# Convolution attention: the first head pair's maxima and the split of wp taken from the start of the attention phase into the end of the projections

## The chip, the cores and the metric

One core of a Trainium2 chip (trn2). The metric is the device time of one execution in microseconds; lower is better. The kernel before took 3423.76 us, the median of three runs (3422.56 to 3425.62).

## The reference

Input x is (8, 768, 32, 32) float32, here used as 8 batches of 768 channels by 1024 positions, with four 768x768 weights. Group normalisation without scale (32 groups, eps 1e-5), then

```python
q, k, v = conv1x1(Wq), conv1x1(Wk), conv1x1(Wv)      # of the normalised x, 12 heads of 64 channels
scores = einsum('bhdn,bhdm->bhnm', q, k) / sqrt(64)
attn = softmax(scores, axis=-1)
out = einsum('bhnm,bhdm->bhdn', attn, v)
return x + einsum('oc,bchw->bohw', Wp, out)
```

## The kernel before, in words

The kernel keeps float32 precision with products of two parts: each operand is split into a rounded part (fp32r, "hi") and the rest ("lo"), and three of the four products are summed. It has two phases, each one block in which every engine runs a program of its own; a barrier stands between them, and tensors of the first phase are freed for the second.

**project_phase.** Eight batches (the first and the last written out, the six between them in a loop), each of two halves of 512 positions. A half is 20 groups: 6 of queries, 6 of keys (18 matmuls of 128x512 each, line 240), 8 of values (18 of 128x384). The groups go round a ring of RING = 4 PSUM banks and of four stage buffers. For a query or key group ACT rounds the bank to the stage's first half (line 290), DVE puts the rest in the second (line 380); for a value group DVE copies (line 385). SP stores to DRAM (q_dram, k_dram at line 175, v_dram at line 179), each after a wait for `lo_done`. The weights lie in `w_hi` and `w_lo`, the normalised input in `xn_hi` and `xn_lo`, with an index for the half. In half 0 the second half of the same batch is normalised on ACT and split on DVE, behind groups 0 to 5, and in half 1 the next batch's first half. The x of the next batch is loaded to `x_raw` in half 0, before group 6's stores. In the last batch there is no next batch. The phase ends when SP has seen all stores land; then comes the barrier (line 49).

**attend_phase.** 48 head pairs (2 heads of 64 channels on the upper and lower 64 rows), each of MT = 8 steps t of 128 keys. For the softmax the kernel needs each query's maximum first. For pair p+1 this is made beside pair p, in UNITS = 16 units: `scores_by_query` (line 731) is two matmuls 64x512, one for each head, to the two banks `rows`, and `unit_max` (line 902) a DVE reduction over both. Unit n waits for the reduction of unit n-1 (`max_done`). When all 16 are done, `join` reduces the halves, turns the result with four 32x32 transposes (lines 908 to 914), and SP sends it as a row to `top` (line 573), one row for each head, whose other rows are zero. `scores_by_key` (line 746) waits for `top_in` at t = 0 and takes, for each step, eight matmuls for each half, the last two of which add the maxima as a product of `ones_r` and `top`. ACT takes the exponent to `p_all` (line 862), POOL sums (line 702), `values` on PE (line 759) multiplies by v. From pair LAG = 8 on, `output` (line 769) multiplies the normalised heads by wp.

PE's order in pair p, step 0, is: unit 0 of pair p+1, then (but for p = 0) the last values of p-1, then unit 1, then scores by key, then unit 2.

**The start of attend_phase before.** SP loads q and k of pair 0, v of pair 0, q and k of pair 1, then wp in five pieces into tensors that are not used yet (lines 562, 563, 567, 644). PE runs pair 0's 16 units, in turn to `rows` and `heads`; DVE clears `ones_r`, `top` and `neg_max` (lines 945 to 947), reduces the 16 units and turns them; SP sends the maxima. ACT rounds wp (line 888), POOL makes its second part (line 710), and SP waits for that (`wp_lo_done`) before it goes on to pair 2's loads; ACT waits for it before the first exponent.

Of the kernel before, what the change touches and what calls it, by code (L numbers as in the profile page):

```python
# [5 lines left out]
F32 = mybir.dt.float32  # L6
# [6 lines left out]
P = 128  # L13
BANK = 512
# [5 lines left out]
def f32(ap):  # L20

    return ap.bitcast(F32)
# [12 lines left out]
def project_phase(nc, S, x, weights, avg_in, q_dram, k_dram, v_dram, psum):  # L35
# [13 lines left out]
    with ExitStack() as ctx:  # L49
# [6 lines left out]
        w_hi = sb("w_hi", [P, 3, KT, C], F32R)  # L56
        w_lo = sb("w_lo", [P, 3, KT, C], F32R)
        x_raw = sb("x_raw", [P, KT, N])
        xn = sb("xn", [P, 2, BANK])
        xn_hi = sb("xn_hi", [P, 2, KT, BANK], F32R)  # L60
        xn_lo = sb("xn_lo", [P, 2, KT, BANK], F32R)
        stage = sb("stage", [P, RING, 2 * BANK], F32R)
        raw = sb("raw", [P, 2, C])
        early = f32(stage[:, :, :]).rearrange("p r n -> p (r n)")[:, 0:EARLY * C].rearrange("p (k o) -> p k o", k=EARLY)
        avg = sb("avg", [P, P])
# [12 lines left out]

        const_in = sem("const_in")
# [25 lines left out]

        NEXT_AT = (0, 2)
# [36 lines left out]
        def _(sp):  # L143
# [39 lines left out]
            for r in range(RING):  # L183
                sp.wait_ge(stored[r], 16 * STORES[r] * S.HALVES * B)

        @block.tensor
        def _(pe):
# [11 lines left out]
            def first_groups():  # L199
                for kt in range(KT):  # L200
                    pe.wait_ge(xn_lo_done, kt + 1)
                    pe.wait_ge(w_hi_done, kt + 1)
                    for g in range(RING):
                        w = w_hi[:, 0, kt, g * P:(g + 1) * P]
                        pe.matmul(psum[:, g, :], w, xn_hi[:, 0, kt, :], start=(kt == 0), stop=False)
                        pe.matmul(psum[:, g, :], w, xn_lo[:, 0, kt, :], start=False, stop=False)
                for g in range(RING):
                    for kt in range(KT):
                        if g == 0:
                            pe.wait_ge(w_lo_done, kt + 1)  # L210
                        mm = pe.matmul(psum[:, g, :], w_lo[:, 0, kt, g * P:(g + 1) * P], xn_hi[:, 0, kt, :], start=False, stop=(kt == KT - 1))
                    mm.then_inc(group_done, 1)

            def project(b, half, last):
# [4 lines left out]
                for g in range(RING if begun else 0, PER_HALF):  # L219
# [3 lines left out]
                    for kt in range(KT):  # L223
# [4 lines left out]
                        a, z = xn_hi[:, half, kt, :], xn_lo[:, half, kt, :]  # L228
                        if g < 2 * KT:
                            w, cols = g // KT, slice(g % KT * P, (g % KT + 1) * P)  # L230
                            wa, wz = w_hi[:, w, kt, cols], w_lo[:, w, kt, cols]
                            parts = [(wa, a), (wa, z), (wz, a)]
                        else:
                            nt, cg = (g - 2 * KT) // 2, (g - 2 * KT) % 2
                            t, cols = slice(nt * P, (nt + 1) * P), slice(cg * VC, (cg + 1) * VC)
                            va, vz = w_hi[:, 2, kt, cols], w_lo[:, 2, kt, cols]
# [4 lines left out]
                    mm.then_inc(group_done, 1)  # L241
                    if half == 0 and not last:
# [15 lines left out]
        def _(act):  # L258
            def high_weights(n):
# [4 lines left out]
                act.copy(w_hi[:, n // KT, n % KT, :], weight_rows(n)).then_inc(w_hi_done, 1)  # L264
# [762 lines left out]
```

## Time and profile before

| what | value |
|---|---|
| median of three runs | 3423.76 us (3422.56 to 3425.62) |
| the profiled execution | 3425.97 us |
| its span (first to last instruction) | 3424.1 us |
| granted clock of TensorE, mean | 0.994 |
| busy share PE / DVE / ACT / POOL | 97% / 52% / 32% / 53% |

All stretches are given in us from the start of the span. The projections take the span to about 1222.6 us, attention the rest. A clock of 1.00 is 2.4 GHz, 0.50 is 1.2 GHz. Matmuls overlap, so the time from the start of one to the start of the next tells more than the length of one.

### The profile page before, as it was taken

How to read it: one execution, taken by the hardware profiler on the slowest of the kernel's cores; microseconds unless marked ns; L12 is line 12 of the kernel's file. 1: busy time of each engine (PE TensorE's matmuls, PEld its weight loads, DVE VectorE, ACT ScalarE, POOL GpSimd, SP SyncE). 2: the span in 40 equal slices, each digit the busy share in tenths (PEclk: the TensorE clock that was granted, in tenths of full speed). 3: DMA queues.
4: the chain of work that ended last, by engine and by line, in shares of the span. 5: the costliest groups of instructions: out<-in, count | busy, mean ns of one | idle time of the engine just before them, and what ended most of it. 6: DMA issues, size and time to landing. Idle time of an engine off the chain costs nothing.

```text
span 3424.1 us, 51515 instructions
## 1 busy us (share of the span) xinstructions
PE 3332.4 (97%) x18272; PEld 2252.0 (66%) x18272; DVE 1784.3 (52%) x2417; ACT 1089.0 (32%) x1944; POOL 1831.8 (53%) x789
## 2 busy tenths in 40 slices
PE   7999999999999979999999999999999999999999
PEld 6888888888888854445555555555555555555557
DVE  5333323333332147775666666666666666666652
ACT  3111111111111114553344444444434444444441
POOL 2000000000000039998888888888888888888883
PEclk9999999999999989999999999999999999999999
DMA  6233333323333332334434434344344344343434
GB/s 233 103 135 111 141 140 115 141 99 135 110 141 111 111 139 88 129 109 157 152 119 154 134 123 159 125 152 158 124 152 148 124 142 146 130 155 124 155 105 166
DMA packets 221695, 461.86 MB, mean 135 GB/s; under 512 B 22960, under 2 KB 73008, under 8 KB 220208
## 3 DMA queue, kind: packets, MB, share of 16 engines
q1 hardware_dynamic: 221488, 459.16, 38.5%
q8 instruction: 123, 2.02, 0.3%
q14 instruction: 84, 0.69, 0.1%
HBM read 259.06 MB, written 199.62 MB: 134 GB/s over the span
## 4 chain that ended last, share of the span: by engine, by line
PE 50%; issue 5%; DVE 5%; DMA 3%; POOL 1%; SPq 1%; ACT 1%; DVEq 0%; ACTq 0%; POOLq 0%
PE psum L746 17%; PE psum L759 16%; PE psum L769 9%; PE psum L731 6%; DVE half_max L902 2%; PE psum L828 1%; DMA recip_rows<-compact 1%; DVE quads L932 1%; DMA top<-turned 1%; DVE compact L935 1%; POOL sums L702 1%; ACT p_all L862 1%; SPq L603 0%; DMA o_parts<-o_lo 0%; POOL o_lo L690 0%
## 5 line engine op out<-in xcount | busy, mean ns | idle before, releaser
L702 POOL TENSOR_TENSOR sums<-sums,p_all 128x1024 f32<-128x1024 f32 x576 | 1350.6, 2378 | 0.0
L902 DVE TENSOR_REDUCE half_max<-psum 128x2 f32<-128x1024 f32 x768 | 935.5, 1220 | 536.4 <-PE psum L731 518.9
L862 ACT ACTIVATE p_all<-psum 128x512 f32<-128x512 f32 x1536 | 793.0, 602 | 948.8 <-PE psum L746 944.1
L759 PE MATMUL psum<-p_all,v 128*64 128x512 f32 x3072 | 743.4, 605 | 0.0
L746 PE MATMUL psum<-q,k 64*128 64x512 f32 x4608 | 672.5, 397 | 13.2 <-DMA top<-turned 10.4
L710 POOL TENSOR_TENSOR wp<-sums,wp 128x1536 fp32r<-128x1536 f32 x1 | 3.5, 3450 | 1177.2 <-ACT wp L888 1177.2
L746 PEld LDWEIGHTS psum<-q,k 64*128 64x128 f32 x4608 | 427.4, 186 | 127.8 <-ACT p_all L862 33.6
L240 PE MATMUL psum<-xn_hi,w_hi 128*128 128x512 f32 x1128 | 439.8, 390 | 1.1 <-DVE stage L380 1.1
L240 PE MATMUL psum<-xn_hi,w_lo 128*128 128x512 f32 x1128 | 439.1, 389 | 0.0
L240 PE MATMUL psum<-xn_lo,w_hi 128*128 128x512 f32 x1128 | 439.0, 389 | 0.0
L290 ACT CAST stage<-psum 128x512 fp32r<-128x512 f32 x192 | 112.4, 587 | 961.4 <-PE psum L240 951.7
L759 PEld LDWEIGHTS psum<-p_all,v 128*64 128x64 f32 x3072 | 186.3, 136 | 345.9 <-issue 295.5
L380 DVE TENSOR_TENSOR stage<-psum,stage 128x512 fp32r<-128x512 f32 x192 | 132.5, 691 | 537.2 <-ACT stage L290 537.0
L731 PE MATMUL psum<-k,q 64*128 64x512 f32 x1536 | 355.8, 459 | 45.3 <-DVE half_max L902 28.6
L702 POOL TENSOR_TENSOR sums<-p_all 128x1024 f32<-128x1024 f32 x96 | 226.4, 2379 | 314.2 <-ACT p_all L862 314.2
L731 PEld LDWEIGHTS psum<-k,q 64*128 64x128 f32 x1536 | 145.7, 186 | 362.3 <-DVE half_max L902 285.9
L769 PE MATMUL psum<-a,wp 128*128 128x512 f32 x1512 | 367.7, 397 | 0.1
L769 PEld LDWEIGHTS psum<-a,wp 128*128 128x128 f32 x1512 | 277.4, 188 | 122.0 <-issue 33.3
L746 PE MATMUL psum<-top,ones_r 64*128 64x512 f32 x1536 | 303.0, 389 | 0.0
L240 PE MATMUL psum<-w_hi,xn_hi 128*128 128x384 f32 x768 | 257.3, 335 | 0.0
L240 PE MATMUL psum<-w_hi,xn_lo 128*128 128x384 f32 x768 | 256.8, 334 | 0.0
L240 PE MATMUL psum<-w_lo,xn_hi 128*128 128x384 f32 x768 | 256.7, 334 | 0.0
(78 smaller groups left out, 2570.1 us busy)
## 6 DMA issues: line engine op xcount, KB each, us to landing
q_parts<-stage SPq DMA_DIRECT2D x192, 256.0 KB, 2.2
k_parts<-stage SPq DMA_DIRECT2D x192, 256.0 KB, 2.3
q<-q_parts SPq DMA_DIRECT2D x48, 1024.0 KB, 5.0
k<-k_parts SPq DMA_DIRECT2D x48, 1024.0 KB, 7.3
a<-o_parts SPq DMA_DIRECT2D x84, 512.0 KB, 7.7
v_rows<-stage SPq DMA_DIRECT2D x128, 192.0 KB, 2.1
v<-v_rows SPq DMA_DIRECT2D x48, 512.0 KB, 4.6
recip_all<-recip_rows SPq DMA_DIRECT2D x96, 256.0 KB, 3.9
```

The lines of the kernel that those rows point to most:

```text
L240: mm = pe.matmul(out, lhs, rhs, start=(kt == 0 and n == 0), stop=(kt == KT - 1 and n == 2))
L290: act.copy(stage[:, r, 0:BANK], psum[:, r, :]).then_inc(hi_done, 1)
L380: dve.tensor_tensor(stage[:, r, BANK:2 * BANK], psum[:, r, :], f32(stage[:, r, 0:BANK]), ALU.subtract).then_inc(lo_done, 1)
L702: pool.tensor_tensor(sums[:, m % 2, i, :], first, p_all[:, i, n, :], ALU.add).then_inc(added, 1)
L731: mm = pe.matmul(to[:, i, :], queries, k[part, e, 0, h * BANK:(h + 1) * BANK], start=True, stop=True)
L746: mm = pe.matmul(psum[:, SCORE_BANKS[2 * h + i], :], left, right, start=(c == 0), stop=(c == 3))
L759: mm = pe.matmul(heads[part, h, :], v[:, e, t, part], p_all[:, i, (m * MT + t) % EXPS, cols], start=(t == 0), stop=(t == MT - 1))
L769: mm = pe.matmul(bank, wp[:, wpart, kt, ot * P:(ot + 1) * P], a_of[kt][:, apart, :], start=first, stop=final)
L828: mm = pe.matmul(psum[:, LAST_BANKS[n], :], wp[:, wpart, kt, ot * P:(ot + 1) * P], a_last[kt][:, apart, half * BANK:(half + 1) * BANK], st ...
L862: act.activation(p_all[:, i, (m * MT + t) % EXPS, h * BANK:(h + 1) * BANK], psum[:, SCORE_BANKS[2 * h + i], :], ACT.Exp, scale=SCALE).then ...
L902: dve.tensor_reduce(half_max[:, :, t, h], of, AX.X, ALU.max, negate=True).then_inc(max_done, 1)
L932: dve.transpose(quads[:, b, :], part[b * SQUARE:(b + 1) * SQUARE, :, :].rearrange("r i c -> r (i c)")).then_inc(quads_done, 1)
```

## The change

The two phases stay two blocks with a barrier. What the second phase's start did is moved into the last half (half 1 of batch 7) of the first, in memory that the last half no longer uses.

- A class `Shared` holds tensors that live through both phases. The weights are now three tensors (queries, keys, values), each with its hi and lo part, and the normalised input two tensors, one for each half. `w_first` (queries) becomes wp; `x_first` (half 0's input) holds slot 0 of q, k and `top`, and slot 1 of `top`; `w_second` (keys) holds slots 1 and 2 of q and k and slot 2 of `top`. The semaphores that pair 0's maxima use are shared too.
- SP: wp is loaded to `x_raw` in the last batch's half 0 before group 6's stores. q and k of pair 0 are loaded at the head of the last half, after a wait for all stores before it; those of pair 1 before group 12's store. Before group 19's store, SP waits for the turned maxima and sends them.
- PE: `maximum_unit` n comes behind group n + 3 of the last half, into PSUM banks 6 and 7, from `x_first`.
- DVE: behind group n + 3's work the reduction of unit n, and behind unit 15 the turn, in the free rows of the buffer `raw`.
- ACT: six copies of wp (768 columns each) behind groups 6 to 11. POOL: the clearing of `top`, and six subtractions for wp's second part.
- From the start of attend_phase go: the loads of q and k of pairs 0 and 1, of wp, the 16 units and reductions, the turn, the memset of `top`, wp's rounding and splitting, and the waits for `wp_lo_done`. v of pair 0 is still loaded there.

The order of PE's instructions around the barrier before. Line 240 is a projection matmul; 731 are units (the 32 matmuls of pair 0's 16 units and the 4 of pair 1's first two stand in one row, x36), 746 scores by key:

```order
L240 MATMUL psum<-w_hi,xn_lo 128x384
L49 UNCONDITIONAL_BRANCH
L718 UNCONDITIONAL_BRANCH
L731 MATMUL psum<-k,q 128x512 x36
L746 MATMUL psum<-q,k 128x512 x6
L746 MATMUL psum<-top,ones_r 128x512 x2
```

And of the change, where line 340 is a projection matmul, 310 a unit of pair 0, 829 a unit of pair 1, 844 scores by key:

```order
L310 MATMUL psum<-x_first 128x512 x2
L340 MATMUL psum<-w_third,x_second 128x384 x18
L106 UNCONDITIONAL_BRANCH
L816 UNCONDITIONAL_BRANCH
L829 MATMUL psum<-w_second 128x512 x4
L844 MATMUL psum<-x_first 128x512 x6
L844 MATMUL psum<-x_first,ones_r 128x512 x2
```

The 32 matmuls now stand in pairs between groups of 18; the last unit has one group behind it.

SP's queue from the last batch on, before:

```order
L175 DMA q_parts<-stage 128x512 x12
L175 DMA k_parts<-stage 128x512 x12
L179 DMA v_rows<-stage 128x3x128 x8
L49 UNCONDITIONAL_BRANCH
L556 UNCONDITIONAL_BRANCH
L562 DMA q<-q_parts 128x2x1024
L563 DMA k<-k_parts 128x2x1024
L567 DMA v<-v_rows 128x1024
L562 DMA q<-q_parts 128x2x1024
L563 DMA k<-k_parts 128x2x1024
L644 DMA sums<-in_wp 128x2x768
```

And of the change, from the last half on (the load of wp stands a half earlier):

```order
L71 DMA x_first<-q_parts 128x2x1024
L72 DMA x_first<-k_parts 128x2x1024
L263 DMA q_parts<-stage 128x512 x12
L263 DMA k_parts<-stage 128x512 x12
L71 DMA w_second<-q_parts 128x2x1024
L72 DMA w_second<-k_parts 128x2x1024
L267 DMA v_rows<-stage 128x3x128 x7
L77 DMA x_first<-turned_first 1x8x128 x2
L267 DMA v_rows<-stage 128x3x128
L106 UNCONDITIONAL_BRANCH
L669 UNCONDITIONAL_BRANCH
L678 DMA v<-v_rows 128x1024
```

Two pairs of loads moved ahead of stores of the last half, and the maxima ahead of its last store.

The diff, cut to its core:

```diff
+class Shared:
...
+        self.w_first = sb("w_first", [P, 2, S.KT, S.C])
+        self.w_second = sb("w_second", [P, 2, S.KT, S.C])
+        self.x_first = sb("x_first", [P, 2, S.KT, BANK])
+        second = self.w_second.rearrange("p a k o -> p (a k o)")
+        first = self.x_first.rearrange("p a k n -> p (a k n)")
+        slots = [first[:, 0:SLOT], second[:, 0:SLOT], second[:, SLOT:2 * SLOT]]
+        self.q = [t.rearrange("p (s a n) -> p s a n", s=2, a=2)[:, 0] for t in slots]
+        self.k = [t.rearrange("p (s a n) -> p s a n", s=2, a=2)[:, 1] for t in slots]
+        self.top = [first[:, SLOT:SLOT + N], first[:, SLOT + N:SLOT + 2 * N], second[:, 2 * SLOT:2 * SLOT + N]]
...
+def load_pair(sp, shared, q_dram, k_dram, p, e):
+    ch = bass.ds(p * P, P)
+    sp.dma_start(f32(shared.q[e]), q_dram[:, ch, :].rearrange("s p n -> p s n")).then_inc(shared.qk_in[e], 16)
+    sp.dma_start(f32(shared.k[e]), k_dram[:, ch, :].rearrange("s p n -> p s n")).then_inc(shared.qk_in[e], 16)
+
+
+def send_maxima(sp, shared, turned, e, MT, DH):
+    for i in range(2):
+        sp.dma_start(f32(shared.top[e][i * DH:i * DH + 1, :]).rearrange("a (t n) -> a t n", t=MT),
+                     f32(turned[i * MT:(i + 1) * MT, :])).then_inc(shared.top_in, 16)
+
+
+def turn_maxima(dve, shared, p, neg_max, flipped, turned, half_max, MT):
+
+    dve.tensor_reduce(neg_max[:, 0:2 * MT].rearrange("p (i t) -> p i t", i=2), half_max[:], AX.X, ALU.min).then_inc(shared.joined, 1)
+    dve.wait_ge(shared.joined, p + 1)
+    for b in range(TURNS):
+        part = slice(b * SQUARE, (b + 1) * SQUARE)
+        dve.transpose(flipped[:, part], neg_max[part, :]).then_inc(shared.flips, 1)
+    dve.wait_ge(shared.flips, TURNS * (p + 1))
+    dve.tensor_reduce(turned[:], flipped[0:2 * MT, :].rearrange("r (n a) -> r n a", a=1), AX.X, ALU.min).then_inc(shared.neg_done, 1)
...
+        w_third = sb("w_third", [P, 2, KT, C], F32R)
+        w_parts = (shared.w_first, shared.w_second, w_third)
+        w_hi, w_lo = [[w[:, part, :, :] for w in w_parts] for part in range(2)]
...
+        turned = sb("turned_first", [2 * S.MT, P], F32R)
...
+        half_max = rest[:, 0:4 * S.MT].rearrange("p (i t h) -> p i t h", i=2, t=S.MT)
+        neg_max = rest[:, 4 * S.MT:4 * S.MT + SQUARE]
+        flipped = rest[0:SQUARE, 4 * S.MT + SQUARE:4 * S.MT + SQUARE + P]
+        wp_raw = x_raw.rearrange("p k n -> p (k n)")[:, 0:KT * C].rearrange("p (k o) -> p k o", k=KT)
+        rows = psum[:, 6:8, :]
...
+        UNIT_AT = 3
+        UNITS = 2 * S.MT
+        LAST_UNIT = B * S.HALVES - 1
...
+                        if last and half == 0 and g == NEXT_AT[0] + KT:
+                            sp.wait_ge(xn_made, B * S.HALVES * KT)
+                            sp.dma_start(wp_raw, wp_rows.rearrange("(k p) o -> p k o", p=P)).then_inc(wp_in, 16)
+                        if last and half == 1 and g == 0:
+                            sp.wait_ge(group_done, LAST_UNIT * PER_HALF)
+                            for r2 in range(RING):
+                                sp.wait_ge(stored[r2], 16 * STORES[r2] * S.HALVES)
+                            load_pair(sp, shared, q_dram, k_dram, 0, 0)
+                        if last and half == 1 and g == 2 * KT:
+                            sp.wait_ge(group_done, LAST_UNIT * PER_HALF + 2 * KT)
+                            load_pair(sp, shared, q_dram, k_dram, 1, 1)
+                        if last and half == 1 and g == PER_HALF - 1:
+                            sp.wait_ge(shared.neg_done, 1)
+                            sp.wait_ge(zero_done, 1)
+                            send_maxima(sp, shared, turned, 0, S.MT, DH)
...
             for r in range(RING):
                 sp.wait_ge(stored[r], 16 * STORES[r] * S.HALVES * B)
+            sp.wait_ge(shared.top_in, 32)
...
+            def maximum_unit(unit):
+                t, h = unit // 2, unit % 2
+                if unit == 0:
+                    pe.wait_ge(shared.qk_in[0], 32)
+                wait(pe, shared.max_done, unit)
+                for i in range(2):
+                    part = slice(i * DH, (i + 1) * DH)
+                    mm = pe.matmul(rows[:, i, :], shared.q[0][part, 0, t * P:(t + 1) * P], shared.k[0][part, 0, h * BANK:(h + 1) * BANK],
+                                   start=True, stop=True)
+                mm.then_inc(shared.rows_ready, 1)
...
+                    if last and half == 1 and 0 <= g - UNIT_AT < UNITS:
+                        maximum_unit(g - UNIT_AT)
...
+                        if last and half == 1 and 0 <= g - KT < KT:
+                            if g == KT:
+                                act.wait_ge(wp_in, 16)
+                            act.wait_ge(group_done, unit * PER_HALF + KT)
+                            act.copy(shared.w_first[:, 0, g - KT, :], wp_raw[:, g - KT, :]).then_inc(wp_hi_done, 1)
...
+            pool.wait_ge(group_done, LAST_UNIT * PER_HALF)
+            pool.memset(f32(shared.top[0]), 0.0).then_inc(zero_done, 1)
+            pool.memset(f32(shared.top[1]), 0.0).then_inc(zero_done, 1)
+            for kt in range(KT):
+                pool.wait_ge(wp_hi_done, kt + 1)
+                pool.tensor_tensor(shared.w_first[:, 1, kt, :], wp_raw[:, kt, :], f32(shared.w_first[:, 0, kt, :]),
+                                   ALU.subtract).then_inc(wp_lo_done, 1)
+            pool.wait_ge(group_done, LAST_UNIT * PER_HALF + 2 * KT)
+            pool.memset(f32(shared.top[2]), 0.0).then_inc(zero_done, 1)
...
+            def unit_max(unit):
+                t, h = unit // 2, unit % 2
+                if unit == 0:
+                    dve.wait_ge(w_lo_done, 3 * KT)
+                    dve.memset(neg_max, 0.0).then_inc(neg_clear, 1)
+                dve.wait_ge(shared.rows_ready, unit + 1)
+                dve.tensor_reduce(half_max[:, :, t, h], rows, AX.X, ALU.max, negate=True).then_inc(shared.max_done, 1)
...
+                        if last and half == 1 and 0 <= g - UNIT_AT < UNITS:
+                            unit_max(g - UNIT_AT)
+                            if g - UNIT_AT == UNITS - 1:
+                                dve.wait_ge(shared.max_done, UNITS)
+                                dve.wait_ge(neg_clear, 1)
+                                turn_maxima(dve, shared, 0, neg_max, flipped, turned, half_max, S.MT)
...
-        q = sb("q", [P, SLOTS, 2, N], F32R)
-        k = sb("k", [P, SLOTS, 2, N], F32R)
-        top = sb("top", [P, SLOTS, N], F32R)
+        q, k, top, wp = shared.q, shared.k, shared.top, shared.w_first
+        qk_in, top_in, rows_ready, max_done = shared.qk_in, shared.top_in, shared.rows_ready, shared.max_done
+        neg_done = shared.neg_done
...
-            load_qk(0, 0, 0)
             load_v(0, 0, 0)
-            load_qk(1, 1, 0)
-            for kts, buf in wp_raw:
-                sp.dma_start(buf, wp_rows[kts.start * P:kts.stop * P, :].rearrange("(k p) o -> p k o", p=P)).then_inc(wp_in, 16)
-            sp.wait_ge(set_done, SETS)
-            maxima(0, 0)
-            sp.wait_ge(wp_lo_done, len(wp_raw))
...
-            for n, (kts, buf) in enumerate(wp_raw):
-                pool.wait_ge(wp_hi_done, n + 1)
-                pool.tensor_tensor(wp[:, 1, kts, :], buf, f32(wp[:, 0, kts, :]), ALU.subtract).then_inc(wp_lo_done, 1)
-            pool.wait_ge(wp_lo_done, len(wp_raw))
...
-            for unit in range(UNITS):
-                scores_by_query(0, 0, None, unit, to=heads if unit % 2 else rows, taken=unit - 1)
...
-                    if known(p) and p == LAG and s == 0:
-                        pe.wait_ge(wp_lo_done, len(wp_raw))
...
-            act.wait_ge(wp_in, 16 * len(wp_raw))
-            for kts, buf in wp_raw:
-                act.copy(wp[:, 0, kts, :], buf).then_inc(wp_hi_done, 1)
-            act.wait_ge(wp_lo_done, len(wp_raw))
...
-            dve.memset(f32(top[:]), 0.0).then_inc(set_done, 1)
             dve.memset(neg_max[:], 0.0).then_inc(set_done, 1)
             dve.wait_ge(set_done, SETS)
-            for unit in range(UNITS):
-                unit_max(0, 0, unit, heads if unit % 2 else rows)
-            join(0, 0)
```

## Rows read from the trace of the kernel before

**Rows 1.** The page's part 1: busy us (share of the span) xinstructions.

```profile
PE 3332.4 (97%) x18272; PEld 2252.0 (66%) x18272; DVE 1784.3 (52%) x2417; ACT 1089.0 (32%) x1944; POOL 1831.8 (53%) x789
```

**Rows 2.** Windows, busy of PE, PEld, DVE, ACT, POOL, then clock, DMA, GB/s.

```profile
1220.00:1230.00 10.00, 2.64 (x16) 2.31 (x14) 3.49 (x5) 0.00 (x0) 0.00 (x0) 0.88 0.44 136
1230.00:1240.00 10.00, 4.40 (x12) 1.65 (x12) 5.50 (x5) 0.00 (x0) 0.00 (x0) 0.50 1.03 414
...
1250.00:1260.00 10.00, 5.63 (x22) 3.39 (x22) 6.40 (x11) 1.81 (x4) 8.53 (x5) 0.50 0.03 7
```

**Rows 3.** The chain of waits at the seam: start, us, what.

```profile
1226.27 7.28 DMA k<-k_parts
...
1234.50 18.20 DVE half_max L902 x16
...
1254.24 0.81 SPq L573
...
1255.09 1.76 DMA top<-turned
...
1256.89 3.78 PE psum L746 x16
1260.68 0.43 PE psum L731 x2
...
1295.07 1.23 PE psum L746 x8
```

**Rows 4.** The timeline at the seam: start, us, engine, line, what [idle before <-releaser].

```profile
1222.30 0.34 PE L240 MATMUL psum<-w_hi,xn_lo 128*128 128x384 f32 x1
1222.67 0.56 DVE L385 COPY stage<-psum 128x384 f32<-128x384 f32 x1 [2.57 <-PE psum L240]
1223.26 0.37 SPq L179 DMA_DIRECT2D v_rows<-stage  x1
1225.83 0.39 SPq L562 DMA_DIRECT2D q<-q_parts  x1
...
1226.67 2.62 DVE L946 MEMSET top<- 128x3072 f32 x1 [0.59 <-issue]
...
1233.59 1.22 PE L731 MATMUL psum<-k,q 64*128 64x512 f32 x4 [10.95 <-DMA k<-k_parts]
```

**Rows 5.** The timeline of DVE, one key group of the last half.

```profile
1198.31 0.69 DVE L380 TENSOR_TENSOR stage<-psum,stage 128x512 fp32r<-128x512 f32 x1 [3.39 <-ACT stage L290]
```

**Rows 6.** The page's part 6: one load of keys, KB, us to landing.

```profile
k<-k_parts SPq DMA_DIRECT2D x48, 1024.0 KB, 7.3
```

**Rows 7.** The timeline of PE at full clock, inside a steady head pair.

```profile
1782.61 0.50 PE L731 MATMUL psum<-k,q 64*128 64x512 f32 x2
1783.04 1.94 PE L759 MATMUL psum<-p_all,v 128*64 128x512 f32 x8
1784.91 4.38 PE L769 MATMUL psum<-a,wp 128*128 128x512 f32 x18
1789.22 0.50 PE L731 MATMUL psum<-k,q 64*128 64x512 f32 x2
```

**Rows 8.** The timeline of POOL, the last of wp's splits.

```profile
1256.72 1.81 POOL L710 TENSOR_TENSOR wp<-v,wp 128x768 fp32r<-128x768 f32 x1
```

**Rows 9.** The timeline of PE: pair 1's first unit, alone.

```profile
1252.84 0.80 PE L731 MATMUL psum<-k,q 64*128 64x512 f32 x2 [1.56 <-DVE half_max L902]
```

**Rows 10.** Windows of 1 us in which the clock fell or rose.

```profile
1227.00:1228.00 1.00, 0.00 (x0) 0.00 (x0) 1.00 (x1) 0.00 (x0) 0.00 (x0) 0.79 0.64 152
1261.00:1262.00 1.00, 1.00 (x10) 0.77 (x8) 0.86 (x1) 0.79 (x2) 0.00 (x0) 0.64 1.06 430
1562.00:1563.00 1.00, 0.00 (x0) 0.00 (x0) 0.00 (x0) 0.00 (x0) 0.13 (x1) 0.54 0.97 168
1568.00:1569.00 1.00, 1.00 (x8) 0.73 (x8) 0.73 (x1) 0.16 (x1) 0.00 (x0) 0.54 0.73 186
```

**Rows 11.** The timeline of PE around the second fall.

```profile
1563.26 0.93 PEld L746 LDWEIGHTS psum<-q,k 64*128 64x128 f32 x6 [3.99 <-DMA top<-turned]
```

More of the change, by code:

```diff
@@ L32, in __init__, with sb, sem @@
         self.NH = self.B * HEADS
-def project_phase(nc, S, x, weights, avg_in, q_dram, k_dram, v_dram, psum):
+SLOTS = 3
+SQUARE = 32
+TURNS = P // SQUARE
+class Shared:
+    def __init__(self, nc, S, ctx):
+        def sb(name, shape):
+            return ctx.enter_context(nc.sbuf_tensor(name, shape, F32R))
+        def sem(name):
+            return ctx.enter_context(nc.semaphore(name))
+        N, SLOT = S.N, 4 * S.N
+        self.w_first = sb("w_first", [P, 2, S.KT, S.C])
[7 more added lines that the diff above has]
+        self.top = [first[:, SLOT:SLOT + N], first[:, SLOT + N:SLOT + 2 * N], second[:, 2 * SLOT:2 * SLOT + N]]
+        self.qk_in = [sem(f"qk_in{s}") for s in range(SLOTS)]
+        self.top_in = sem("top_in")
+        self.rows_ready = sem("rows_ready")
+        self.max_done = sem("max_done")
+        self.joined = sem("joined")
+        self.flips = sem("flips")
+        self.neg_done = sem("neg_done")
@@ L203, in first_groups @@
                     for g in range(RING):
-                        w = w_hi[:, 0, kt, g * P:(g + 1) * P]
-                        pe.matmul(psum[:, g, :], w, xn_hi[:, 0, kt, :], start=(kt == 0), stop=False)
-                        pe.matmul(psum[:, g, :], w, xn_lo[:, 0, kt, :], start=False, stop=False)
+                        w = w_hi[0][:, kt, g * P:(g + 1) * P]
+                        pe.matmul(psum[:, g, :], w, xn_hi[0][:, kt, :], start=(kt == 0), stop=False)
+                        pe.matmul(psum[:, g, :], w, xn_lo[0][:, kt, :], start=False, stop=False)
                 for g in range(RING):
@@ L449, in attend_phase @@
         flipped = sb("flipped", [SQUARE, P])
-        turned = sb("turned", [2 * MT, 2, P], F32R)
+        turned = [sb(f"turned{n}", [2 * MT, P], F32R) for n in range(2)]
         flip = sb("flip", [P, N])
@@ L571, in maxima @@
                 sp.wait_ge(neg_done, p + 1)
-                for i in range(2):
-                    sp.dma_start(f32(top[i * DH:i * DH + 1, m % SLOTS, :]).rearrange("a (t n) -> a t n", t=MT),
-                                 f32(turned[i * MT:(i + 1) * MT, m % 2, :])).then_inc(top_in, 16)
+                send_maxima(sp, shared, turned[m % 2], m % SLOTS, MT, DH)
             def spread_recip(p):
@@ L721, in _, with scores_by_query @@
             PRODUCTS = [(kt, wpart, apart) for kt in range(KT) for wpart, apart in ((0, 0), (0, 1), (1, 0))]
-            def scores_by_query(p, m, u, unit, to=rows, taken=None):
+            def scores_by_query(p, m, u, unit):
                 t, h = unit // 2, unit % 2
@@ L727, in scores_by_query @@
                     pe.wait_ge(qk_in[e], 32 * (turn(p, m, u) + 1))
-                wait(pe, max_done, p * UNITS + unit if taken is None else taken)
+                wait(pe, max_done, p * UNITS + unit)
                 for i, part in enumerate(half_of):
-                    queries = q[part, e, 0, t * P:(t + 1) * P]
-                    mm = pe.matmul(to[:, i, :], queries, k[part, e, 0, h * BANK:(h + 1) * BANK], start=True, stop=True)
+                    queries = q[e][part, 0, t * P:(t + 1) * P]
+                    mm = pe.matmul(rows[:, i, :], queries, k[e][part, 0, h * BANK:(h + 1) * BANK], start=True, stop=True)
                 mm.then_inc(rows_ready, 1)
@@ L896, in _, with unit_max @@
         def _(dve):
-            def unit_max(p, m, unit, of=rows):
+            def unit_max(p, m, unit):
                 t, h = unit // 2, unit % 2
@@ L901, in unit_max @@
                     wait(dve, neg_done, p)
[L902 removed]
+                dve.tensor_reduce(half_max[:, :, t, h], rows, AX.X, ALU.max, negate=True).then_inc(max_done, 1)
             def join(p, m):
```

79 lines of the change are left out of this document (29 added, 50 removed).

## The prediction

> **What bounds the kernel now.** I read the page first, then the windows, then the chain of waits, then the timelines at the seam. PE is busy 97% of the span [rows 1], so little can be won except where PE stands still. The windows show where that is: the seam between the two phases. From 1220 to 1230 us PE works 2.64 us of 10, from 1230 to 1240 4.40, from 1250 to 1260 5.63, the last two at a granted clock of 0.50, which is 1.2 GHz [rows 2]. The chain says what the seam waits for, in order: the transfer of the first pair's keys (7.28 us, to 1233.54), sixteen row maxima on DVE (18.20 us), the turning of the maxima, their two transfers (the first issued at 1254.24, the second landing 1.76 us after 1255.09), and at 1256.89 the first scores by key [rows 3]. The last projection ends on PE at 1222.64 [rows 4]. So the seam, from the last projection to the first scores by key, is 1256.89 - 1222.64 = 34.25 us. From 1256.89 on the work is the same before and after the change, so its new length is the whole question.
>
> **What the change moves, and its price.** The sum follows the moment of the first score by key.
>
> 1. *The loads of pair 0 leave the seam.* They are issued on SP at the head of the last half, 16.3 us before their first use: a key or query group takes 0.69 + 3.39 = 4.08 us [rows 5], and the first unit stands behind the fourth. SP first waits for the stores of the half before. Such a store is issued 0.6 us after its group, and in the old seam issue, landing and barrier together took 1225.83 - 1223.26 = 2.57 us [rows 4], so SP goes on about 3.2 us into the half. Queries and keys need a median of 7.3 us [rows 6], which makes 11 us of the 16.3. Cost nothing; without that cover PE would wait for the difference. The stores of the half's first group, now behind these two DMAs in SP's queue, are only issued from 5 us on anyway. Pair 1's loads sit before the first value group, 27 us or more before their use.
>
> 2. *Sixteen units (two matmuls each) enter the last half on PE.* That time is added, since PE has no gap there. The nearest row is a unit between 128-row matmuls at full clock: 1783.04 - 1782.61 = 0.43 us [rows 7]. Cheapest would be 0.24, half of one of the eight pairs in 3.78 us at half clock [rows 3]. Dearest: the 18 matmuls ahead of a unit took 4.31 us [rows 7] against a projection group's 4.08, 0.23 more, so 0.66. I take 0.49, near the first row. 16 x 0.49 = 7.8 us; ends 3.8 and 10.6. The Trainium skill, TensorEngine Tiling (Array Packing), section Key Properties, says that changing the tiling mode drains the engine. If each unit then cost what a lone pair did, 0.80 us at half clock [rows 9], the sum would be 5.0 us dearer, a rival below; the row above shows 0.2 us over the bare pair, so the trace bears out a mild form only.
>
> 3. *Their maxima on DVE.* A unit's reduction takes 18.20 / 16 = 1.14 us in the old seam, and DVE is idle 3.39 us of each 4.08 [rows 5], 2.57 us of each 3.13 in value groups [rows 4]. Cost nothing: the next unit comes a group later, and PE is four banks ahead.
>
> 4. *wp.* One load of 2.36 MB, in the place where other batches load x; six copies on ACT and six splits on POOL of 1.81 us [rows 8], all idle then. They were beside the maxima before, the last split ending at 1258.53, so they pay back nothing either.
>
> 5. *The block's end.* Old: 1225.83 - 1222.64 = 3.19 us from PE's end to SP's first instruction behind the barrier. New: behind group 18 come unit 15 on PE, its maximum and the turn. From the reduction's end at 1252.70 to SP's issue at 1254.24 this took 1.54 us [rows 3]. So: unit 0.5, reduction 1.2, turn 1.5, two issues of 0.81; SP is free for the last value store 4.9 us behind group 18. The last group ends 0.49 + 3.13 = 3.6 us behind it, so the store goes 1.25 us after PE's end where it went 0.62 before [rows 4]. Then 2.57 us as before: 3.8 us, 0.6 more. The top rows land meanwhile (1.76 us after the second issue).
>
> 6. *The new block's start.* PE waits for two DVE memsets. Old DVE showed 0.59 us of issue gap before the second, which began 0.84 us after SP's first instruction [rows 4]; I take 1.0 us, without the 2.62 us memset of `top`, which is on POOL and hidden. Then unit 0 of pair 1, at half clock: 0.91 us to the reduction's start (1233.59 to 1234.50), 1.23 us of reduction and a step of 0.05, 2.2 us in all; then unit 1 and 0.43 us to the scores by key [rows 3]. The old seam had these two units as well, the first at 1252.84 [rows 9], spread around the turn.
>
> Sum: 7.8 + 3.8 + 1.0 + 2.2 + 0.4 = 15.2 us in place of 34.25, so 19.0 us less. The profiled execution took 3425.97 us with a span of 3424.1; less 19.0 is 3407.0. The median of the three runs is 3423.76, 2.2 below that execution, and the forecast is made against it: **3404.8 us**. Every number above is a difference, so the offset carries over.
>
> *The clock.* A window of 1 us at a mean of 0.79 was at full rate for 0.58 of it and at half for the rest, so the clock fell at 1227.58, 4.9 us after PE's last matmul; in the same way it rose at 1261.7, 4.8 us into the dense scores [rows 10]. At the other fall PE had stopped at 1563.26 - 3.68 = 1559.58 [rows 11]; the clock fell at 1562.1, 2.5 us later, and rose at 1568.9. The new PE stands still 4.8 us (3.8 + 1.0), then works thinly. I assume that it falls again and that the same half-speed stretch follows, so it adds nothing to the difference. What is late next is the barrier itself and the two memsets; from the first scores on, PE.
>
> **The rivals.**
>
> *The clock holds.* For it: 4.9 us of idleness in one case were needed, and the new stop is 4.8. Against: the other took 2.5. Then the half-rate stretch of 4.8 us costs 2.4 less, and unit and reduction about 0.5 less: 3401.9.
>
> *The units drain PE.* A lone pair took 0.80 us. 16 x 0.80 = 12.8, 5.0 more: 3409.8. Against it stands 0.43 at full clock.
>
> *PE's first instruction behind the barrier is late.* Before, PE had 1233.59 - 1225.83 = 7.76 us in which to get ready under the DMA wait; it now has 1.0. At most 6.8 us would come out: 3411.6. DVE's 0.59 us gap speaks for a little of it. The Trainium skill, Runtime: NRT & Kernel Launch, section Instruction fetch mechanics, states that a taken branch whose target isn't held forces a fetch first. No row shows PE's.
>
> *It does not do what it says.* The stores wait behind 4 MB of new loads, the ring of four stage buffers runs out and PE stalls in the last half for what the seam gives back, 12 us or more of the 19: about 3421. Against: two loads are some 5 us of transfer at 414 GB/s [rows 2], and the ring holds four groups, 16 us.
>
> *Slower: pair 0 runs at half clock.* With 4.40 us of work in 10 the clock stayed at 0.50 in the old seam [rows 2]. If the shorter lead-in left pair 0 without its rise, a stretch of t us at 1.2 GHz would lose t/2, and once it is 38 us longer than the old one the gain is gone. Pair 0 took 1295.07 - 1256.89 = 38.2 us [rows 3]; all of it at half rate would add up to 38 - 2.4 = 35.8, so 35.8 - 19.0 = 16.8 over the old time: 3440.6. Against: the scores run dense from the first on, and in both cases the clock rose within 5.7 us of their start [rows 10, 11].
>
> **How the numbers follow.** Forecast 0.69, clock holds 0.14, drained units 0.06, late PE 0.06, no gain 0.03, slower 0.02. The likeliest case alone reaches from 3400.8 (units at 0.24) to 3407.6 (0.66), and a median of three moves by 1.5. With the holding clock below and the drained or late start above, the range is 3399.5 to 3411.5. Against what a measurement can tell, 0.2% or 6.8 us: faster 0.95, same 0.03, slower 0.02.
>
> **What would show it.** In the changed profile: sixteen units of two matmuls in the last half with no wait for DVE or DMA, groups 0.4 to 0.6 us longer; PE's end near 1230.4; SP's first instruction of the second phase near 1234.2; first scores by key near 1237.9; pair 1's first scores by key 38 us after those of pair 0, as before. Wrong would be: a PE wait for the keys' load inside the last half, a unit that costs over 0.7 us, or a gap on PE behind the barrier over 2 us with the memsets done. The forecast falls if the first scores by key come later than 1245.

## The result

The changed kernel took 3429.49 us (median of 20 runs, 3427.57 to 3432.68), the kernel before, measured beside it, 3423.84 us (3420.12 to 3425.89): a ratio of 1.0017 with a 95% interval of 1.001 to 1.0023. The change made the kernel slower by some 5.7 us; 19 us less had been forecast. The profiled execution has a span of 3430.7 us, against 3424.1 before. A ratio leaves out executions over 1.5% above the fastest of their kernel; two of all that follow are such, both of the version with the other engines shifted. From the page of the changed kernel, the engines' busy times and the queue that carries PE's instructions:

```profile
PE 3341.6 (97%) x18272; PEld 2253.6 (66%) x18272; DVE 1779.4 (52%) x2417; ACT 1089.2 (32%) x1945; POOL 1835.5 (54%) x793
...
q8 instruction: 127, 2.08, 0.3%
```

**The seam did what was forecast.** The windows of the changed kernel around the phase change, as [rows 2] of before:

```profile
1220.00:1230.00 10.00, 10.00 (x56) 8.96 (x55) 4.11 (x5) 0.00 (x0) 0.00 (x0) 1.00 0.21 59
1230.00:1240.00 10.00, 4.58 (x26) 3.50 (x24) 4.94 (x12) 0.00 (x0) 0.00 (x0) 0.94 0.27 77
1250.00:1260.00 10.00, 10.00 (x71) 5.55 (x68) 5.70 (x5) 4.79 (x10) 10.00 (x6) 1.00 0.00 0
```

From 1250 us on PE is full, where before it was still half idle. The timeline at the same place, as [rows 4]:

```profile
1231.78 2.25 PE L340 MATMUL psum<-w_third,x_second 128*128 128x384 f32 x12
...
1235.04 0.43 SPq L267 DMA_DIRECT2D v_rows<-stage  x1
1237.71 0.36 SPq L678 DMA_DIRECT2D v<-v_rows  x1
...
1238.06 0.50 PE L829 MATMUL psum<-w_second 64*128 64x512 f32 x2 [4.04 <-DVE neg_max L1030]
...
1239.95 0.80 PE L829 MATMUL psum<-w_second 64*128 64x512 f32 x2 [1.38 <-DVE half_max L992]
...
1240.54 1.48 PE L844 MATMUL psum<-x_first 64*128 64x512 f32 x6
```

And from the chain of waits there, as [rows 3]:

```profile
1240.74 3.41 PE psum L844 x16
```

PE ends at 1231.78 + 2.25 = 1234.03, SP's first instruction behind the barrier comes 3.7 us later (3.8 forecast), PE's 0.35 us after that (1.0), the two units are 1.9 us apart (2.2), and the scores by key begin at 1240.74 by the chain of waits; before it was 1256.89. What the units cost in the last half is read from DVE's groups, as [rows 5]:

```profile
1166.72 0.69 DVE L505 TENSOR_TENSOR stage<-psum,stage 128x512 fp32r<-128x512 f32 x1 [3.39 <-ACT stage L392]
...
1171.46 0.69 DVE L505 TENSOR_TENSOR stage<-psum,stage 128x512 fp32r<-128x512 f32 x1 [2.90 <-ACT stage L392]
...
1222.80 0.56 DVE L510 COPY stage<-psum 128x384 f32<-128x384 f32 x1 [2.06 <-PE psum L340]
...
1226.55 0.56 DVE L510 COPY stage<-psum 128x384 f32<-128x384 f32 x1 [2.06 <-PE psum L340]
```

A query or key group with a unit takes 1171.46 - 1166.72 = 4.74 us in place of 4.08, a value group 3.75 in place of 3.13. A unit costs 0.64 us, and 16 cost 10.3 us. The seam with the units' price is then 10.3 + 1240.74 - 1234.03 = 17.0 us, against 34.25: 17.2 us gained, of 19.0 forecast.

**The loss lies elsewhere, in four places.** The transfers of a pair's maxima mark the pairs. Up to the one sent at 1990.98 us the changed kernel is ahead by 17.35 us. The next pair loses 5.6. From the timelines of SP, first before, then changed:

```profile
2008.33 1.70 SPq L573 DMA_DIRECT2D top<-turned  x2
...
2055.09 1.40 SPq L573 DMA_DIRECT2D top<-turned  x2
```

```profile
1990.98 1.54 SPq L77 DMA_DIRECT2D x_first<-turned  x2
...
2043.37 1.41 SPq L77 DMA_DIRECT2D x_first<-turned  x2
```

2055.09 - 2008.33 = 46.76 us, 2043.37 - 1990.98 = 52.39 us. The same happens three times more, six pairs apart each time (6.2, 6.4 and 6.3 us), and from the second pair on nowhere else by more than 1 us; together 24.5 us. Pairs 12 to 41 are a loop of six pairs, run five times, and each of these places is its turn, the four times where every engine branches back. PE there, first before, then changed:

```profile
2005.41 1.94 PE L759 MATMUL psum<-p_all,v 128*64 128x512 f32 x8
2008.95 0.50 PE L731 MATMUL psum<-k,q 64*128 64x512 f32 x2 [1.60 <-issue]
2009.38 1.94 PE L759 MATMUL psum<-p_all,v 128*64 128x512 f32 x8
2011.25 4.37 PE L769 MATMUL psum<-a,wp 128*128 128x512 f32 x18
```

```profile
1988.05 1.94 PE L857 MATMUL psum<-p_all,v 128*64 128x512 f32 x8
1994.81 0.80 PE L829 MATMUL psum<-w_second 64*128 64x512 f32 x2 [4.82 <-issue]
1995.54 3.68 PE L857 MATMUL psum<-p_all,v 128*64 128x512 f32 x8
1999.14 4.77 PE L867 MATMUL psum<-a,w_first 128*128 128x512 f32 x18
```

After the branch PE stands still for 1.60 us before and for 4.82 us now, and both stops are put down to "issue": nothing that the profile shows was missing. In the changed kernel the clock falls meanwhile; the window in which it does:

```profile
1993.00:1994.00 1.00, 0.00 (x0) 0.00 (x0) 0.00 (x0) 0.00 (x0) 1.00 (x1) 0.62 0.03 5
```

So the two matmuls of the unit take 0.80 us in place of 0.50, the eight of L857 3.68 in place of 1.94, and the next 18 4.77 in place of 4.37. With 3.22 us of longer stop that is 5.7 us, the 5.6 of this pair. The page names a suspect: PE's instruction queue (q8) moved 127 blocks where it moved 123 before, four more for four turns:

```profile
q8 instruction: 123, 2.02, 0.3%
```

The trace has the time of each of these fetches, and they fit the stops. Before, blocks begin to come at 2005.87 and 2009.41 us, and PE goes on at 2008.95, 3.1 us after the first. In the changed kernel they begin at 1989.13, 1992.12 and 1998.79, and PE goes on at 1994.81 only, 2.7 us after the second. The view of the DMA queues for 1989 to 1990 and for 1992 to 1993 us has one block each:

```profile
q8 instruction: 1, 0.02, 6.0%
q8 instruction: 1, 0.02, 6.7%
```

### The profile page after: what moved, and what is told of

It reads as the page before. It is cut to its first block, busy times and chain, and to the rows that moved or that the text cites. A ratio compares the mean times of both kernels' runs of the same rounds, so it can differ in the third digit from the quotient of the medians.

```text
span 3430.7 us, 51516 instructions
## 1 busy us (share of the span) xinstructions
PE 3341.6 (97%) x18272; PEld 2253.6 (66%) x18272; DVE 1779.4 (52%) x2417; ACT 1089.2 (32%) x1945; POOL 1835.5 (54%) x793
## 4 chain that ended last, share of the span: by engine, by line
PE 51%; issue 5%; DVE 4%; POOL 1%; DMA 1%; ACT 1%; SPq 0%; DVEq 0%; ACTq 0%; POOLq 0%
PE psum L844 17%; PE psum L857 16%; PE psum L867 10%; PE psum L829 6%; DVE half_max L992 2%; PE psum L922 1%; DVE quads L1016 1%; POOL sums L804 1%; DVE compact L1019 1%; ACT p_all L956 1%; DMA recip_rows<-compact 0%; DVE compact L1021 0%; DMA w_second<-turned 0%; SPq L712 0%; DMA x_first<-turned 0%
## 5 line engine op out<-in xcount | busy, mean ns | idle before, releaser
L857 PE MATMUL psum<-p_all,v 128*64 128x512 f32 x3072 | 750.4, 610 | 0.0
L844 PE MATMUL psum<-w_second 64*128 64x512 f32 x3072 | 447.9, 396 | 9.4 <-DMA w_second<-turned 5.5
L857 PEld LDWEIGHTS psum<-p_all,v 128*64 128x64 f32 x3072 | 187.4, 137 | 349.2 <-issue 298.3
L867 PE MATMUL psum<-a,w_first 128*128 128x512 f32 x1512 | 371.3, 399 | 0.2 <-DMA a<-o_parts 0.2
L867 PEld LDWEIGHTS psum<-a,w_first 128*128 128x128 f32 x1512 | 279.8, 189 | 126.4 <-issue 36.5
L844 PEld LDWEIGHTS psum<-w_second 64*128 64x128 f32 x3072 | 284.5, 185 | 86.2 <-ACT p_all L956 24.2
L829 PE MATMUL psum<-w_second 64*128 64x512 f32 x1024 | 234.8, 454 | 38.0 <-issue 19.1
L829 PEld LDWEIGHTS psum<-w_second 64*128 64x128 f32 x1024 | 96.5, 184 | 249.2 <-DVE half_max L992 186.3
L844 PE MATMUL psum<-x_first 64*128 64x512 f32 x1536 | 224.5, 397 | 2.0 <-DMA x_first<-turned 1.4
L340 PE MATMUL psum<-w_third,x_first 128*128 128x384 f32 x1152 | 203.1, 335 | 0.3 <-DVE stage L505 0.3
L340 PE MATMUL psum<-w_third,x_second 128*128 128x384 f32 x1152 | 203.2, 335 | 0.0
L844 PE MATMUL psum<-x_first,ones_r 64*128 64x512 f32 x1024 | 201.6, 389 | 0.0
L340 PEld LDWEIGHTS psum<-w_third,x_second 128*128 128x128 f32 x1152 | 199.7, 188 | 2.5 <-issue 2.0
L340 PEld LDWEIGHTS psum<-w_third,x_first 128*128 128x128 f32 x1152 | 199.8, 188 | 1.2 <-DVE stage L505 0.6
```

The costliest lines, as they stand in the source:

```text
L340: mm = pe.matmul(out, lhs, rhs, start=(kt == 0 and n == 0), stop=(kt == KT - 1 and n == 2))
L829: mm = pe.matmul(rows[:, i, :], queries, k[e][part, 0, h * BANK:(h + 1) * BANK], start=True, stop=True)
L844: mm = pe.matmul(psum[:, SCORE_BANKS[2 * h + i], :], left, right, start=(c == 0), stop=(c == 3))
L857: mm = pe.matmul(heads[part, h, :], v[:, e, t, part], p_all[:, i, (m * MT + t) % EXPS, cols], start=(t == 0), stop=(t == MT - 1))
L867: mm = pe.matmul(bank, wp[:, wpart, kt, ot * P:(ot + 1) * P], a_of[kt][:, apart, :], start=first, stop=final)
```

## The experiments

**Theory A**, formed on this: PE's instructions come by DMA in blocks (2.02 MB in 123, so 16 KB each). A backward branch to a block that PE no longer holds must first fetch it; where only the last places of that block are left to run, PE must wait for the next block too. The change moved the loop's place in PE's program: 32 matmuls left the second phase and came to the first, which keeps the sum, but the wait for `wp_lo_done` at pair 8 went, an instruction of its own. Counting PE's instructions in the built programs (each matmul with its weight load as two), the loop begins at number 9410 before and 9409 now; its body has 2938 instructions in both. The Trainium skill (Runtime: NRT & Kernel Launch, Instruction fetch mechanics) states blocks of 256 instructions and a stall at a taken branch whose target isn't held; the size agrees with the 16 KB here, at 64 bytes each. **Theory B**: the new places of q, k, top and wp, or the order of the loads, disturb the loop. **Theory C**: some other engine's program crosses a block.

### One instruction more on PE

```diff
                     wait(pe, y_done, (p - LAG) * 2 + s)
+                    if known(p) and p == LAG and s == 0:
+                        for _ in range(1):
+                            pe.wait_ge(set_done, SETS)
```

> The changed kernel with one instruction more on PE ahead of the attention loop: a second, already satisfied wait for set_done before the first output group of pair 8. It brings the loop's first PE instruction back to the place in PE's program (number 9410, with weight loads counted) that it has in the kernel before; the change had moved it to 9409. Theory A (PE's instruction fetch at the loop's backward branch): the four stops of PE at the loop's turn fall from 4.4 to 5.0 us to 1.2 to 1.6 us, the clock doesn't drop there, PE's queue fetches 123 blocks and not 127, and the time is 3405 to 3409 us, 22 us under the changed kernel. Theory B (the new places of q, k, top and wp in memory, or the new order of loads, slow the loop): one more wait changes nothing, 3429 us. Theory C (another engine's program crosses a block now): 3429 us too.

Measured: 3408.08 us (3405.52 to 3409.11), ratio to before 0.9946 (0.9932 to 0.9961), 21 us under the changed kernel. The medians put it 15.9 us under the kernel before (3423.98 us in this comparison). Its page and the first turn on PE:

```profile
q8 instruction: 123, 2.02, 0.2%
```

```profile
1987.91 1.94 PE L857 MATMUL psum<-p_all,v 128*64 128x512 f32 x8
1990.96 0.50 PE L829 MATMUL psum<-w_second 64*128 64x512 f32 x2 [1.11 <-issue]
1991.39 1.94 PE L857 MATMUL psum<-p_all,v 128*64 128x512 f32 x8
```

The stop is 1.11 us (the four are 1.11, 1.48, 1.20 and 1.50), L857 takes 1.94 us, and 123 blocks are fetched. A single wait that was already satisfied brought back most of the 17.2 us that the change had won at the seam. Theories B and C fall.

### One instruction less in the kernel before

```diff
-                    if known(p) and p == LAG and s == 0:
-                        pe.wait_ge(wp_lo_done, len(wp_raw))
```

> The kernel before with one instruction less on PE ahead of the loop: the wait for wp_lo_done before the first output group of pair 8 is left out (ACT and SP wait for the same thing long before). Nothing of the change is in it. Theory A: the loop's first PE instruction is number 9409 as in the changed kernel, and each of the four turns costs 5.7 us more: 3446 us, 127 blocks fetched. Theories B and C: 3424 us.

Measured: 3445.74 us (3443.39 to 3446.87), ratio 1.0056 (1.0041 to 1.0071): 21.8 us slower by the medians, from the removal of a wait. Page and first turn:

```profile
q8 instruction: 127, 2.08, 0.3%
```

```profile
2003.85 1.94 PE L759 MATMUL psum<-p_all,v 128*64 128x512 f32 x8
2010.77 0.80 PE L731 MATMUL psum<-k,q 64*128 64x512 f32 x2 [4.98 <-issue]
2011.49 3.68 PE L759 MATMUL psum<-p_all,v 128*64 128x512 f32 x8
```

The other kernel shows the same: a stop of 4.98 us and the half clock behind it. Nothing of the change but this one line is in it.

### Seventeen more, and three more

The same edit with 33 waits and with 5. In the built programs two such waits stand in one instruction, so these make 17 and 3.

> The changed kernel with 33 more waits of the same kind, which make 17 instructions on PE. Theory A, in the form that only the last places of a fetched block are bad: as with one instruction more, 3405 to 3409 us, turns of 1.2 to 1.6 us. Were it a matter of hitting one exact number: slow again, 3429 us.

> The changed kernel with 5 waits more, which make 3 instructions on PE: the loop's first instruction is number 9412 and its end 12350 (one instruction more: 9410 and 12348, 3408.1 us, 123 blocks; seventeen more: 9426 and 12364, 3412.2 us, 127 blocks). If only the loop's start against the border of a block counts, 3408 us. If its end counts as well and a border lies between 12348 and 12350: 3412 us and 127 blocks; if that border lies further on: 3408 us and 123 blocks.

Measured: with 17, 3412.16 us (3409.51 to 3414.16), ratio 0.996 (0.9947 to 0.9974); with 3, 3407.15 us (3405.74 to 3409.99), ratio 0.9947 (0.9934 to 0.9961). With 17, 127 blocks were fetched and the first turn's stop was:

```profile
q8 instruction: 127, 2.08, 0.3%
```

```profile
1991.84 0.49 PE L829 MATMUL psum<-w_second 64*128 64x512 f32 x2 [1.89 <-issue]
```

The four stops are 1.66 to 1.89 us, not 4 to 5, so it is no matter of one exact number. The time missed its forecast of 3405 to 3409 us: it lies 4 us above the version with one instruction, more than the stops alone explain (0.45 us each). Behind the first turn's stop of 1.89 us the clock falls here too, as this window shows, which is at 1.00 with one instruction:

```profile
1993.00:1997.00 4.00, 4.00 (x12) 1.85 (x9) 1.23 (x1) 1.01 (x1) 1.71 (x1) 0.57 0.67 224
```

In its trace one block more is fetched just before each turn, which three more instructions do not bring (123 blocks, stops of 1.14 to 1.66): the end of the loop seems to count a little as well, through a block that is fetched ahead and not used. That reading was not tested further. So a count of 127 blocks alone does not mean long stops.

### The other engines shifted

Six waits more on DVE, ACT and POOL each and four on SP ahead of the loop, PE as in the changed kernel:

```diff
+            for _ in range(6):
+                dve.wait_ge(set_done, SETS)
             all_pairs(dve, pair)
```

> The changed kernel with 6 more waits each on DVE, ACT and POOL (3 instructions each) and 4 on SP (2 instructions) ahead of the loop, PE's program untouched. Theory A: nothing moves, 3429 us, turns of 4.4 to 5.0 us. Theory C: the four turns are cheap again and the time is near 3407 us.

Measured: 3426.5 us, the median of eight executions (3423.94 to 3428.89); two more took 3706.31 and 8326.67 us, and the median of all ten is 3427.08. The ratio is 1.0002 (0.9992 to 1.0013). The four turns keep their stops (4.25 to 5.09 us), the first of them:

```profile
1994.73 0.80 PE L833 MATMUL psum<-w_second 64*128 64x512 f32 x2 [5.09 <-issue]
```

The time is 3.0 us under the changed kernel's, which was measured in another comparison, so the other engines' places may be worth a little; the 21 us aren't there.

### Forty-one and nine places left in the block

Once more the first edit, with 431 and 495 waits, to put the loop's start near the end of a block on purpose.

> The changed kernel with 431 more waits on PE ahead of pair 8's first output group (216 instructions): the loop's first instruction is number 9625. If blocks of 256 begin at 9410, 41 instructions of the target's block are left to run, some 20 matmuls or 4.6 us. Theory A: the next block (fetched 3 us after the first) is there in time, so the loop's turns cost 1.1 to 2 us, as at 9410, 9412 and 9426. 127 blocks, since the loop then touches one more. The added waits themselves cost PE some us once, at pair 8.

> The same with 495 more waits (248 instructions): number 9657, 9 instructions left in its block, at most four matmuls or 0.9 us. Theory A: PE runs those few and then stands still until the second block is there: two stops at each turn, in all 3.5 to 4.5 us, with or without a fall of the clock. If only the very last place of a block were bad: turns of 1.1 to 2 us.

One run each, beside 3425.72 us for the kernel before: 3425.8 and 3445.88 us. Both carry the added waits themselves, which PE runs through at pair 8; this row of the first shows it stopped there for 20.83 us. That is 96 ns for each of the 216 instructions; the second stopped for 24.25 us, with 32 instructions more. By the pairs' marks it cost less, 15.7 us, as a wait of 3.48 us for the pair's maxima, which the changed kernel has there, is now hidden behind it. Then the first one's first turn:

```profile
1557.84 6.29 PE L867 MATMUL psum<-a,w_first 128*128 128x512 f32 x18 [20.83 <-issue]
```

```profile
2006.63 0.50 PE L829 MATMUL psum<-w_second 64*128 64x512 f32 x2 [1.53 <-issue]
2007.06 1.94 PE L857 MATMUL psum<-p_all,v 128*64 128x512 f32 x8
```

And the first turn with nine places left:

```profile
2007.93 1.94 PE L857 MATMUL psum<-p_all,v 128*64 128x512 f32 x8
2011.21 0.50 PE L829 MATMUL psum<-w_second 64*128 64x512 f32 x2 [1.34 <-issue]
2011.64 0.64 PE L857 MATMUL psum<-p_all,v 128*64 128x512 f32 x1
2014.24 2.82 PE L857 MATMUL psum<-p_all,v 128*64 128x512 f32 x5 [1.96 <-issue]
```

With 41 left the turns stop PE for 1.48 to 1.61 us, once each. Both versions fetch 128 blocks, where 127 were expected. With nine left it stops for 1.34 us, runs a unit and one matmul, and stops again for 1.96 us, then has the half clock: two waits for two blocks, seen apart. The blocks begin to come at 2008.31 and 2011.64, 2.9 and 2.6 us before PE goes on. The forecast held in kind, two stops at each turn; together they are 3.30, 3.45, 3.86 and 3.50 us, where 3.5 to 4.5 were expected, and the clock falls at three of the four turns.

### Only the loads early

To part the gain at the seam: loads, wp and zeros of `top` as in the change, the units, maxima and turn back at the start of the attention phase (loop at 9410). In short:

```diff
-                    if last and half == 1 and 0 <= g - UNIT_AT < UNITS:
-                        maximum_unit(g - UNIT_AT)
...
+            for unit in range(UNITS):
+                scores_by_query(0, 0, None, unit, to=heads if unit % 2 else rows, taken=unit - 1)
             pe.wait_ge(set_done, SETS)
```

> Only a part of the change: the loads of q and k of pairs 0 and 1, wp and the zeros of top stay in the last half, but pair 0's sixteen units, their maxima and the turn stand at the start of the attention phase, as in the kernel before (loop at 9410). The seam then is 3.2 us (block end) + 0.4 + 0.9 (first unit at half clock) + 18.2 (maxima) + 1.5 (turn) + 2.7 (transfers) = 26.9 us in place of 34.25: 3416.6 us. So the early loads would be worth 7.4 us and the early units 9.9 us of the change's 17.2 at the seam. If the loads were hidden by something else anyway: 3424 us.

Measured: 3416.74 us (3414.39 to 3418.0), ratio 0.9973 (0.9963 to 0.9984), 8.1 us under before. Its chain of waits:

```profile
1227.58 18.20 DVE half_max L986 x16
...
1249.99 3.78 PE psum L833 x16
```

The sixteen maxima take their 18.20 us again, as in [rows 3], only 6.9 us earlier. The seam is 26.2 us (PE ends at 1223.76), where 26.9 were expected. So the loads (with wp and the zeros) were worth 8 us. Moving the units was worth another 7.8 us, by each version's distance from the kernel before in its own comparison (15.9 and 8.1), less than the 9.9 expected: 10.3 us of added PE time replace DVE's 18.2, the turn and its transfers.

### Two units a visit

The version with one instruction more; units 2j and 2j+1 behind group 3 + 2j, the odd ones in PSUM banks 4 and 5.

```diff
-                    if last and half == 1 and 0 <= g - UNIT_AT < UNITS:
-                        maximum_unit(g - UNIT_AT)
+                    if last and half == 1 and 0 <= g - UNIT_AT < UNITS and (g - UNIT_AT) % 2 == 0:
+                        maximum_unit(g - UNIT_AT)
+                        maximum_unit(g - UNIT_AT + 1)
```

> The changed kernel with the one PE instruction more (loop at 9410), and its sixteen units in eight visits of two: units 2j and 2j+1 behind group 3+2j, the second in PSUM banks 4 and 5, which the last batch doesn't use. Theory A (a unit costs its 0.23 us and some 0.41 us of change between 128-row and 64-row matmuls, paid for each visit): a visit of two costs 0.87 us, eight 7.0 us where sixteen single ones cost 10.2; the maxima are turned two groups earlier, so SP's last store isn't held up: 0.6 us. In all 3.8 us under the kernel with one instruction more (3408.1): 3404.3 us. Rival (the cost lies in each unit's own two matmuls and waits): eight visits of 1.28 us, 3408 us. Loop turns 1.1 to 1.5 us.

Measured: 3403.51 us (3403.06 to 3407.19), ratio 0.9938 (0.9925 to 0.9952), the kernel before in this comparison at 3424.81. That is 4.6 us under the version with one instruction more, where 3.8 were expected. DVE in the value groups, with and without a visit:

```profile
1205.90 0.56 DVE L511 COPY stage<-psum 128x384 f32<-128x384 f32 x1 [0.41 <-PE psum L340]
1209.03 0.56 DVE L511 COPY stage<-psum 128x384 f32<-128x384 f32 x1 [2.57 <-PE psum L340]
1209.50 2.35 DVE L486 TENSOR_REDUCE raw<-psum 128x2 f32<-128x1024 f32 x2
1213.02 0.56 DVE L511 COPY stage<-psum 128x384 f32<-128x384 f32 x1 [1.18 <-PE psum L340]
```

A group with two units takes 1213.02 - 1209.03 = 3.99 us, one without 3.13: 0.86 us for a visit of two, where two single visits cost 1.28. A unit's own part is then 0.22, the visit's 0.42.

### Maxima sent one store earlier

```diff
-                        if last and half == 1 and g == PER_HALF - 1:
+                        if last and half == 1 and g == PER_HALF - 2:
```

> The kernel of two units a visit, with the turned maxima sent before group 18's store and not before group 19's. If SP's two issues (1.5 us) in front of the last store still hold up the block's end, it gains up to 0.6 us: 3403.7. If the last store was free already, as the turn ends two groups earlier: no difference, 3404.3.

Measured: 3403.74 us (3401.62 to 3404.45), ratio 0.9936 (0.9922 to 0.9949), no difference from the version above. SP's last store was already free. These two beat both the kernel before and the changed one.

## Why the prediction was wrong

**The step that failed** is the sentence under "What bounds the kernel now": "From 1256.89 on the work is the same before and after the change, so its new length is the whole question." The work was the same, its time was not: 24.5 us came at the four turns of the loop. The term was missing from the sum, and the slower rival named another mechanism and place (pair 0 at half clock); the clock was back at 1.00 some 5 us after pair 0's first scores, as before. The nearest thing in the prediction was the rival of a late first instruction on PE, which had the right mechanism, a fetch after a taken branch, at the wrong branch: behind the barrier PE started after 0.35 us. The turns lay open in the trace of before, as stops of 1.15 to 1.60 us without a releaser; they had not been read, since the windows were searched only where the change works. The exact cost, though, needed the count of PE's instructions too.

Point by point:

- *Loads hidden:* right. PE waits for no DMA in the last half. With only these moved, the gain was 8.1 us.
- *Units at 0.49 us:* too low, 0.64 measured, inside the bounds of 0.24 and 0.66: 10.3 us for 7.8. The upper bound, which adds what the 18 128x128 matmuls ahead of a unit took above a projection group, came out nearly right. This term is the one that was mis-sized at the seam, by 2.5 us in all. The two-unit visit shows that 0.42 us are paid once a visit. That they are the price of changing the tile shape is the likely reading; no run tests it apart.
- *Maxima, wp, zeros:* right, no wait for them shows.
- *Block's end and start:* 3.7 us for 3.8, then 0.35 us for 1.0; unit to unit 1.9 us for 2.2, as the clock still stood at 2.4 GHz for the first; then 0.8 us to the scores by the chain, for 0.4. PE's last projection ended at 1234.03 us, not near 1230.4: 2.5 us of that are the dearer units, 1.1 us it was late before the last half.
- *The clock falls at the seam:* right, 4.9 us after PE's last projection; it was still at 1.00 when the first unit began (0.50 us for its two matmuls, 0.80 for the next).
- *Sum at the seam:* 17.2 us, for 19.0. With the loop back in its place the kernel takes 3408.08 us, inside the stated range of 3399.5 to 3411.5; so the forecast had the effect of the edit and missed that of its side effect.

## What to carry to other kernels

Removing or adding a single instruction ahead of a long loop can move its start over the border of a fetched block: here one wait was worth 21 us in both directions, more than the change itself. Where a loop's body is so long that its blocks are fetched again at each turn (2938 instructions here), look in the trace at each turn for a stop without a releaser and for what the instruction queue fetches there. If the stops are long, pad ahead of the loop with a satisfied wait (one sufficed here). A count of blocks that rose by one a turn is a hint and no proof: two versions with short stops had it too. Small matmuls of another tile shape are cheaper between large ones if they come two at a visit.

## What was not expected of the hardware

- At the attention loop's turns PE stood still for 1.1 to 1.9 us where it waited for one block, and for 4.1 to 5.1 us where it waited for two one after the other. Then the clock fell to 1.2 GHz as well, and a turn lost 4.2 to 6.4 us in all.
- The projections' loop, 1498 instructions by the same count, costs PE nothing at its five turns: its matmuls run on without a stop at 322.3 us and at the four turns behind it, and from 310 to 1070 us the instruction queue moves no block at all, before and in the changed kernel. So PE kept the whole body, which is nearly six blocks.
- With nine instructions left in the block both waits are seen apart; with 41 left the second is hidden.
- A stretch of satisfied waits stopped PE for some 96 ns for each instruction of two waits, with whatever block had to be fetched in it.
- In the profiled executions the clock's first rise came between 25.6 and 27.2 us in runs whose code up to there is the same. The changed kernel's first value group was 1.2 us behind that of the kernel before (84.15 against 82.94 us on DVE), long before the last half.
